# Layer 1's ring of Q, K, V, x and top-value buffers: four places in place of three

## What is computed

```python
q_lat, k_lat, v_lat = x @ Wq_down, x @ Wk_down, x @ Wv_down      # 16 heads x 64
q = concat([q_c, rope(q_e)]); k = concat([k_c, rope(k_e)])       # 8 per head
att = softmax(causal(q @ k.T / sqrt(8))); y = (att @ v) @ Wc
# experts: logits = x @ wg; the two best of 128; place = running count in the expert
# buf[expert, place] = x;  yb = buf @ we;  y = g1 * yb[idx1] + g2 * yb[idx2]
```

## Time and profile before

| What | us |
|---|---|
| median of three runs | 2201.09 |
| profiled execution | 2217.88 |
| its span, first to last instruction | 2216.1 |
| layer 1's part of the span | about 1448 to 2216 |

### The profile page before, as it was taken

How to read it: one execution, slowest core, us unless ns; L and a number is a source line. 1 busy time by engine, 2 the same in 40 slices (tenths; PEclk the granted TensorE clock), 3 DMA queues, 4 the chain that set the end, 5 groups by cost and what they waited for, 6 DMA issues and landing times. The chain is left out here.

```text
span 2216.1 us, 40363 instructions
## 1 busy us (share of the span) xinstructions
PE 1973.5 (89%) x13618; PEld 1134.9 (51%) x13618; DVE 1736.0 (78%) x2778; ACT 1343.3 (61%) x2423; POOL 1293.1 (58%) x975
## 2 busy tenths in 40 slices
PE   5799999999999999999999999948999999988886
PEld 3455555555555555555555555534555555544442
DVE  5699988998898898898888988838877677764445
ACT  3577677776776776776777777513555555534443
POOL 2486876876777867767777768643332222215540
PEclk7899999999999999999999999958999999988887
DMA  8541532523515515415335235052322222233437
GB/s 203 140 103 43 138 89 63 134 68 89 133 41 117 125 30 136 103 44 137 84 68 133 72 79 134 6 147 93 101 88 82 79 85 84 86 100 111 123 96 234
DMA packets 184476, 222.49 MB, mean 100 GB/s; under 512 B 28632, under 2 KB 122880, under 8 KB 180160
## 3 DMA queue, kind: packets, MB, share of 16 engines
q1 hardware_dynamic: 179568, 215.29, 37.8%
q0 software_dynamic: 2048, 4.18, 0.7%
q10 hardware_dynamic: 2640, 0.24, 0.1%
HBM read 165.41 MB, written 54.27 MB: 99 GB/s over the span
## 5 line engine op out<-in xcount | busy, mean ns | idle before, releaser
L732 POOL TENSOR_TENSOR dBx<-REP,BC 128x1024 f32<-128x1024 f32 x256 | 603.2, 2359 | 281.9 <-DVE dA L897 223.3
L897 DVE TENSOR_TENSOR_SCAN dA<-dA,dBx 128x512 f32<-128x512 f32 x512 | 626.2, 1223 | 108.5 <-POOL dBx L732 67.0
L404 PE MATMUL UP<-xnT,W 128*128 128x512 f32 x1024 | 518.4, 624 | 57.3 <-ACT hT L606 43.2
L413 PEld LDWEIGHTS DN<-W,hT 128*128 128x128 f32 x4096 | 469.7, 192 | 110.9 <-issue 100.6
L413 PE MATMUL DN<-W,hT 128*128 128x128 f32 x4096 | 496.4, 278 | 0.3 <-ACT GD L613 0.3
L597 ACT ACTIVATE dA<-REP,A 128x512 f32<-128x512 f32 x512 | 354.2, 695 | 89.9 <-DVE PR L906 81.7
L606 ACT ACTIVATE hT<-UP,b 128x512 f32<-128x512 f32 x512 | 355.2, 694 | 75.1 <-PE UP L404 67.9
L906 DVE TENSOR_TENSOR PR<-dA,BC 128x512 f32<-128x512 f32 x512 | 353.6, 691 | 31.5 <-DVE dA L897 18.8
L404 PEld LDWEIGHTS UP<-xnT,W 128*128 128x128 f32 x1024 | 179.3, 194 | 284.5 <-issue 146.5
L1802 DVE TENSOR_REDUCE NM<-S 128x4 f32<-128x1024 f32 (+1 forms) x192 | 234.2, 1220 | 113.0 <-PE S L1355 44.5
L1557 ACT ACTIVATE PT<-S 128x1024 f32<-128x1024 f32 x192 | 196.8, 1025 | 111.0 <-PE S L1377 52.5
(11 more groups left out here) (256 smaller groups left out, 2768.3 us busy)
## 6 DMA issues: line engine op xcount, KB each, us to landing
BC<-s_b SPq DMA_DIRECT2D x128, 256.0 KB, 6.4
REP<-s_dx SPq DMA_DIRECT2D x124, 256.0 KB, 7.5
REP<-s_delta SPq DMA_DIRECT2D x124, 256.0 KB, 8.0
s_parts<-SPL SPq DMA_DIRECT2D x32, 384.0 KB
s_dx<-tz SPq DMA_DIRECT2D x16, 512.0 KB, 3.1
s_y<-zeros SPq DMA_DIRECT2D x32, 256.0 KB, 5.2
YC<-s_y SPq DMA_DIRECT2D x16, 512.0 KB, 5.6
s_delta<-soft SPq DMA_DIRECT2D x32, 255.0 KB, 3.1
```

The lines of the kernel that those rows point to most:

```text
L404: nc.tensor.matmul(UP[k % 2][:], W1[:, e % E0, f * P:(f + 1) * P], xnT[:, q, :], start=True, stop=True).then_inc(upf.sem, 1)
L413: last = nc.tensor.matmul(DN[:, j * P:(j + 1) * P], hT[:, e % 2, f, j * P:(j + 1) * P], W2[:, e, f, :], start=(f == 0), stop=(f == FB - 1))
L732: nc.gpsimd.tensor_tensor(dBx[:, s % 2], DX[:, h, j:j + 2, :], BC[:, q // 2, q % 2, :].unsqueeze(1).to_broadcast([P, 2, T0]), ALU.mult).th ...
L897: nc.vector.tensor_tensor_scan(h, h, dBx[:, k // 2 % 2, k % 2, :], 0.0, ALU.mult, ALU.add).then_inc(scan_done.sem, 1)
```

## The change

`BUF` goes from 3 to 4. By it the tiles `XN2`, `QS`, `KS`, `V`, `mx` and `ix` and the scratch tensors `s_parts` and `s_nm` get a fourth place, `xnT2` a twelfth, `poolset` and `xn_stored` are counted to the new number, and each wait with `n - BUF` looks four sequences back. No transfer, no computation and no place in the schedule changes, but for one more fill of a `V` and one of a `KS` place at the start of the layer.

```diff
 SCALE = 1.0 / float(np.sqrt(DH))
 E1, CAP = 128, 32
-BUF = 3
+BUF = 4
 LEAD = 4
 UNITS = 6
```

## The result

The changed kernel takes 2178.03 us (median of four runs, 2175.72 to 2181.44). The kernel before, run beside it, takes 2202.36 us (four runs, 2199.76 to 2203.68). The ratio is 0.9888, with a 95% interval of 0.9874 to 0.9903: a gain of 24.3 us where 20.0 was forecast. The profiled execution of the changed kernel took 2175.72 us, its span is 2173.9 us.

The account below looks back on a forecast made before the run. In the middle stage PE was held by late `QS` loads, in a ring through SP's wait for second passes. 13.3 + 2.4 + 2.9 + 1.8 - 0.4 = 20.0 us off the 2201.09 us median gave 2181 us, range 2169 to 2197.

Parts of the forecast that it names:

- The wait at L1274: Layer 1, SP before the load: the wait for the second pass of n-3, 1.21 us per sequence, falls away.
- The size in the middle: Middle stage: PE's wait at L1351 falls from 1.48 to 0.65 us in 16 sequences, a gain of 13.3 us.
- the law by which I got 0.65: Middle stage: two waits plus 18.2 us of PE work equal the 19.5 us store chain, so s = 0.65 us.
- the other loop: Middle stage: chain from L1351's start through the store of the maxima, 18.6 us, giving s = 0.4 us.
- Cover on other engines: Middle stage: ACT work done during PE's wait stays in time; costed at nothing, 3 us if that cover goes.
- The late stage: Late layer 1: shorter load waits give 2.4 us for sequence 24 and 2.9 us for the other four.
- The clock: After sequence 24's wait: 10.2 us at half clock cost some 3.7 us; half, 1.8 us, comes back.
- The early stage and the start: Layer 1: nothing gained early; one more KS and V fill on POOL loses 0.4 us, between 0 and 2.3.
- the slower rival: The earlier load meets other traffic, landing later than 7.9 us after the last issue: 2217 us; chance 0.06.
- the new wait: The store's landing becomes last, at 4.37 us restoring the old wait: 2198 us; chance 0.16 together with no effect.
- the rival of a larger gain: SP's full 19.4 us, 5 from other late waits and 3.7 of clock come through: 30.1 us, 2171; chance 0.16.

Follow-up runs that it names:

- first trace: First profiled execution of either kernel, nothing else altered: the kernel before took 2217.88 us, the changed kernel 2175.72 us.
- The moved store chain: ACT's second cast, POOL's sum and subtraction and SP's store half a slot earlier for all sequences, against the changed kernel: 2203.42 us, ratio 0.9911.
- its own test: Three small loads of 8 KB added on SP ahead of the 12 loads, against the changed kernel: 2219.94 us, ratio 1.0063.
- third trace: Kernel before, unchanged, profiled a third time on one chip beside the changed kernel: 2204.48 us, ratio 1.0.
- the first four kernels: Kernel before again, four places with old wait, four places for scores' buffers alone, store's chain earlier; the kernel before takes 2220.32 us on their chip.

## Why the prediction held, step by step

**The wait at L1274.** Right, and shown from both sides: the old wait alone takes the whole gain away, and the ring of the scores' buffers alone gives the middle stage its gain. The buffers for V, x, norm and top values bring nothing that can be measured: with them at three and the scores' ring at five, the middle takes 282.3 us and the late stage 192.6.

**The size in the middle.** Right. Forecast: a wait of 0.65 us a sequence and a period of 18.9. Measured: 10.7 us in 16 sequences, 0.67 each (the single waits at L1351 added up, first trace), and 284.5 / 15 = 18.97 and 282.2 / 15 = 18.82. The 12.1 us stand against 13.3 because that sum had 16 periods and T(7) to T(22) are 15, which is 12.5. The moved store chain, which takes the last wait away, shows the chain's role. That the added wait halves, the law by which I got 0.65, was not confirmed by its own test: when the chain was lengthened the other loop had already taken over. I had computed that loop (18.6 us, s = 0.4) and dropped it as shorter, without saying how narrow the range was in which it stays so. What supports the law within that range is the changed kernel's own chain, whose store follows PE's stop by the same 2.9 us for waits from 0.3 to 1.0.

**Cover on other engines.** Costed at nothing. PE's busy time in the middle is 272.76 before and 272.78 after, and nothing of ACT's cover was missed.

**The late stage.** This is the step that failed in size. The forecast had 2.4 + 2.9 for waits and 1.8 for the clock, 7.1 us; the pair on one chip gives 9.1 and 6.6 in the two rows, 14.9 in the time and 1.7 more after T(31). Two things went wrong. First, I costed the waits one by one, and gave the full 2.4 us only to sequence 24, where it could be read off. But the late stage has the same ring as the middle. Timelines of SP and PE, first of the kernel before (third trace), then of the changed kernel:

```profile
2050.88 0.60 PE L1351 MATMUL S<-maskq,identb 128*128 128x512 bf16 x2 [3.14 <-DMA QS<-s_parts]
2057.82 0.39 PE L1385 MATMUL S<-maskk,identb 128*128 128x256 bf16 x2
2058.24 3.83 SPq L1261 DMA_DIRECT2D KS<-s_parts  x6
```

```profile
2031.66 0.61 PE L1351 MATMUL S<-maskq,identb 128*128 128x512 bf16 x2 [1.95 <-DMA QS<-s_parts]
2033.61 0.42 SPq L1270 DMA_DIRECT2D s_parts<-SPL  x1
2036.59 3.85 SPq L1261 DMA_DIRECT2D KS<-s_parts  x6
2052.18 0.61 PE L1351 MATMUL S<-maskq,identb 128*128 128x512 bf16 x2 [2.10 <-DMA QS<-s_parts]
```

Before, the load starts 7.36 us after L1351, held by L1385; changed, 4.93 us, held by the store. That is the same 2.4 us as for sequence 24, in a period of 20.5 us where it was 22.9. Second, the execution on which I built is one whose late stage hides this. There PE waited for the loads only 12.6 us in five waits, in the third trace 27.0 in eight. In the first trace ACT, PE and DVE (3.57 us, where the third has 1.32) stood together at places where the third has shorter gaps or none. ACT and PE near 2022 us of the first trace, then the same instructions in the third (the last column is the idle time before):

```profile
2022.16 0.58 ACT L1551 COPY OSB<-OT 128x512 f32<-128x512 f32 x1 [5.09 <-remote]
2022.80 1.11 PE L1501 MATMUL EP<-ident,OSB 128*128 128x128 f32 x4 [2.78 <-ACT OSB L1551]
```

```profile
2018.07 0.59 ACT L1551 COPY OSB<-OT 128x512 f32<-128x512 f32 x1 [1.75 <-PE OT L1401]
2019.11 0.60 PE L1501 MATMUL EP<-ident,OSB 128*128 128x128 f32 x4
```

That execution was 16.8 us above the median, and I had weighed these 16.8 us as if they could sit in the waits that the sum lives on. They sat in the late stage and hid such waits there: it takes 222.9 us in the first trace, 231.0 in the second and 208.9 in the third, while the middle is the same within 2.3 us. It fits that on the chip of the first four kernels, where the kernel before takes 2220 us, the scores' ring alone gained 13.5 us by its ratio (11.8 by the medians), while with five places it gained 27.5 us (29.8) on the second chip. What makes the three engines stand together stays open.

**The clock.** The direction was right, 1.8 us was too little. PE's busy time late fell by 6.6 us, and the control with the old wait for late sequences brings it back (0.87, 178.12 us). I had priced one stretch after sequence 24; in the third trace of the kernel before each of the eight late waits, of 3.0 to 4.0 us, is followed by a stretch at half clock, of 3.4 to 13.7 us. A clock of 0.89 over 208.9 us is 46 us at half clock, 0.93 over 194.1 is 27; the 19 us between, at my 0.36 us each, make 6.8. The Trainium skill ("TensorE: Matmul & The Clock Gate", "HAM oscillation — how this bites in real kernels") has the rule that waits for DMA between bursts of matmuls cost clock. The trace agrees for waits of about 3 us and does not for those of 1.5 us.

**The early stage and the start.** No change early, as forecast (146.4 and 146.9 us). The two added fills on POOL, `V` and `KS` of the changed kernel, and the first rotary sum, beside the earlier trace rows:

```profile
1451.88 1.28 POOL L1592 MEMSET V<- 128x288 f32 x4
...
1458.13 7.04 POOL L1611 MEMSET KS<- 128x2048 bf16 x4
1465.13 1.26 POOL L1615 TENSOR_TENSOR t<-t 128x512 f32<-128x512 f32 x1
```

The `KS` fill ends as the rotary sum can start: covered. The fourth `V` fill takes 0.3 us and not 0.5, and lies ahead of a wait for DVE that has room for it. From the first `V` fill to the rotary sum are 13.25 us; in the third trace of the kernel before they are 12.95. So the start costs at most 0.3 us. That T(0) came 2.9 us later in the pair is not this: there POOL's first `V` fill already starts 3.3 us later (1452.32 and 1455.66), which is layer 0, and between the two traces of the changed kernel T(0) differs by 3.5 us as well.

**The rivals.** A slow store came once in the middle (sequence 11, 4.3 us from issue to L1276, and PE then stood 1.71 us), as that rival has it, but not as a rule. In the middle, where PE waited for the loads, the first pass started at most 6.3 us after the last issue, never near 7.9, so the slower rival found no ground. The Trainium skill's rule of a higher DRAM latency under load ("DMA: Bandwidth & Descriptors", "Latency and other measured facts"), which I had set beside the new wait, found none there either: with the DMA engines busy for 0.28 of the time the landing did not grow. The result lies between the forecast and the rival of a larger gain, for a reason that neither had: the late stage.

## What to carry to other kernels

A buffer's depth pays only through the wait that it moves, so find what is late next on the same queue, follow it back to the engine that waits, and write each closed loop as a sum; keep all loops whose sums are close, since the gain ends where the next one takes over. When the same loop runs through several stages, price it by stage and by period, also where a single profiled execution shows other stalls in its place. Before building on a profiled execution that is longer than the median, find in which stage the excess lies.

## What the runs showed of the hardware

- Waits and the clock: PE's granted clock stayed at 1.00 with waits of 1.3 to 1.6 us in each period of 19.6 us (in the first trace one period out of 15 had 0.92). It was 0.97 in a stage whose waits averaged 1.85 us; there it fell after waits of 1.8, 2.4, 2.8 and 3.1 us and not after others of 2.2 to 2.6. It was 0.88 with waits of 2.8 to 3.2 us every 21 to 24 us. In the last, every wait was followed by a stretch at half clock, in 12 of 16 periods from the first matmuls on (1.04 us for the L1356 pair in place of 0.60).
- Three extra DMAs of 8 KB each on SP's queue took 1.23 us to issue in most periods, some 0.4 us each; the kernel took 41 us more with them, 25.1 of it in the middle stage and 12.3 in the late one.
- The kernel before took 2203.75 and 2206.19 us on two chips and 2220.32 on a third. The changed kernel was not run on the third; the scores' ring alone had a ratio of 0.9939 there, the changed kernel 0.9893 on the first. The late stage of the kernel before took 208.9 us in one trace and 222.9 and 231.0 in two others, so its gain depends on what else stands there; whether that goes with the chip is not shown.
